# TensorE issues the values of four slots in one block instead of two

## What is computed

```
content  = einsum('bhqd,bhkd->bhqk', q, k)
relative = einsum('bhqd,qkd->bhqk', q, rel_k[idx])      # idx = clip(k - q, -128, 128) + 128
w        = softmax((content + relative) / sqrt(8))
out      = einsum('bhqk,bhkd->bhqd', w, v) + einsum('bhqk,qkd->bhqd', w, rel_v[idx])
x = x + layernorm(out @ Wo.T + bo)
x = x + layernorm(ffn(layernorm(x)))                    # shared expert + the one routed expert
```

## Time and profile before

| | |
|---|---|
| median of three runs | 1906.22 us |
| span of the profiled execution, first to last instruction | 1789.6 us |
| what lies around the span in the median run | 116.6 us |
| TensorE busy | 1620.7 us, 91% of the span |
| TensorE weight loads busy | 1354.0 us, 76% |
| VectorE busy | 1256.6 us, 70% |
| ScalarE busy | 1116.0 us, 62% |
| mean granted TensorE clock | 0.974 |

### The profile page before, as it was taken

One profiled execution on the slowest core, in us unless ns is written; L12 is line 12 of the kernel. 1 busy time (PEld: TensorE's weight loads), 2 busy tenths in 40 slices (PEclk: granted clock), 3 DMA queues, 4 the chain that ended last, 5 costly groups with the idle time before them and its releaser, 6 DMA issues. The chain is left out here.

```text
span 1789.6 us, 72871 instructions
## 1 busy us (share of the span) xinstructions
PE 1620.7 (91%) x28157; PEld 1354.0 (76%) x28157; DVE 1256.6 (70%) x3502; ACT 1116.0 (62%) x2060; POOL 540.0 (30%) x1114
## 2 busy tenths in 40 slices
PE   2889999999999999999999899999999989976991
PEld 1668888888878878887878788888888776555991
DVE  5996658787868776877787768787777234523994
ACT  3337676766766667666766676767656665325880
POOL 5422121413131313131413132313101112770566
PEclk9999999999999999999999999999999999997996
DMA  2478864775454445444544364446433652324451
GB/s 56 128 193 205 171 144 104 172 164 153 90 137 95 124 92 149 78 127 95 153 68 128 80 133 98 117 94 140 95 67 77 151 159 58 123 76 113 140 159 44
DMA packets 490909, 212.47 MB, mean 119 GB/s; under 512 B 332392, under 2 KB 464165, under 8 KB 490561
## 3 DMA queue, kind: packets, MB, share of 16 engines
q1 hardware_dynamic: 475968, 165.76, 41.9%
q0 software_dynamic: 14592, 42.00, 7.1%
HBM read 105.73 MB, written 102.85 MB: 117 GB/s over the span
## 5 line engine op out<-in xcount | busy, mean ns | idle before, releaser
L936 ACT ACTIVATE w<-sc,escale 128x512 f32<-128x512 f32 x1024 | 691.6, 688 | 425.2 <-PE sc L734 271.2
L1137 DVE TENSOR_REDUCE mx<-mix 128x1 f32<-128x512 f32 x960 | 649.0, 686 | 274.0 <-PE mix L713 221.8
L727 PE MATMUL sc<-QC,KC 104*128 104x128 f16 x4096 | 401.0, 221 | 16.1 <-issue 11.8
L753 PE MATMUL pv<-w,VC 128*9 128x128 f32 x8192 | 381.1, 275 | 1.8 <-DVE rel_s L1151 1.8
L727 PEld LDWEIGHTS sc<-QC,KC 104*128 104x128 f16 x4096 | 262.9, 99 | 131.2 <-issue 85.4
L708 PE MATMUL mix<-WE 128*128 128x367 f16 (+2 forms) x960 | 312.0, 325 | 24.4 <-DVE mx L1137 16.2
L709 PE MATMUL mix<-Wn,WE 128*128 128x367 f16 (+2 forms) x960 | 284.5, 296 | 1.1 <-issue 1.1
L927 ACT ACTIVATE WE<-qp,hmask 128x256 f16<-128x256 f16 x512 | 249.4, 501 | 23.9 <-PE sc L711 14.7
L734 PE MATMUL sc<-QT,Wt 96*128 96x64 f16 x5120 | 259.3, 192 | 3.5 <-issue 3.4
L760 PE MATMUL rel<-w,Rv 128*32 128x128 f32 x5120 | 260.6, 274 | 1.7 <-issue 1.7
L753 PEld LDWEIGHTS pv<-w,VC 128*9 128x9 f32 x8192 | 174.7, 90 | 62.2 <-issue 43.6
(11 more groups left out here) (232 smaller groups left out, 2130.3 us busy)
## 6 DMA issues: line engine op xcount, KB each, us to landing
qm_d<-ks POOLq DMA_DIRECT2D x48, 512.0 KB, 4.6
QT<-qm_d SPq DMA_DIRECT2D x32, 768.0 KB
kt_d<-ks SPq DMA_DIRECT2D x48, 256.0 KB
KC<-kt_d SPq DMA_DIRECT2D x128, 96.0 KB
xs_d<-zrow SPq DMA_DIRECT2D x5, 2056.0 KB, 12.1
vs_d<-vst SPq DMA_DIRECT2D x16, 576.0 KB, 5.4
VC<-vs_d SPq DMA_DIRECT2D x32, 288.0 KB
orl_d<-rel_s SPq DMA_DIRECT2D x512, 8.0 KB
```

Of the source, the lines that this page charges most:

```text
L727: mm = nc.tensor.matmul(bank[:, P * g:P * g + P], KC[j][:, b2, g, 0 if near else 1, :], qc[:, g, :, 32 * q8:32 * q8 + 32], start=(g == 0), ...
L753: mm = nc.tensor.matmul(pv[b2][32 * g:32 * g + 9, P * hh:P * hh + P], VC[j][:, b2, 0 if near else 1, h, :], wt[:, :, b2, h, :], start=(j = ...
L936: nc.scalar.activation(w[tile % 2][:, slot % 4, slot // 4 % 2].rearrange("p h q -> p (h q)"), sc[slot % 2][:], ACT.Exp, scale=escale[:, 0: ...
L1137: nc.vector.tensor_reduce(mx[:, k:k + 1], nat[:], AX.X, ALU.max).then_inc(s["mx_done"], 1)
```

## The change

The values of four slots are issued together in every fourth slot (3, 7, 11, ...), where the values of two slots were issued in every second.

```diff
-                if slot % 2 == 1:
-                    for earlier in (slot - 1, slot):
+                if slot % 4 == 3:
+                    for earlier in range(slot - 3, slot + 1):
                         if slot >= 8:
                             values(i, slot // 8 - 1, earlier % 8)
                         elif prev:
                             values(i - 1, 15, earlier)
```

## The result

| | before | after |
|---|---|---|
| median of four runs each, same comparison | 1907.39 us (1903.23 to 1922.66) | 1933.55 us (1931.20 to 1938.91) |
| ratio, 95% interval | | 1.0123 [1.0082, 1.0165] |
| span of a profiled execution on such a chip | 1898.9 us | 1932.5 us |
| the seven turns with sets, first to last | 1270.6 us | 1283.5 us |
| last turn, first scores to last values | 131.1 us | 145.7 us |

The changed kernel is slower by 1.2%, 23 to 26 us. The prediction was 1921 us in a range of 1897 to 1937.

The account below looks back on a forecast made before the run. TensorE was taken to set the pace. The last turn's +11.3 us and the seven turns' +3.5 us (border gains against new waits) sum to +14.8 us, 1921 us by the median, in a range of 1897 to 1937.

Parts of the forecast that it names:

- Border, 0.20 us a block: Entering and leaving each block of values on TensorE costs 0.20 us; 256 fewer blocks, gross gain 5.8 us a turn.
- Last turn, gross +16.0: Without sets to fill the burst, exponentials set the pace; all four kinds of group lengthen, 16.0 us together.
- Last turn, less 4.7 hidden behind DMAs: TensorE's waits for output DMAs at slots 41 and 100 hide 1.8 and 2.9 us, leaving +11.3 us.
- Seven turns, new waits group by group: In turns with sets, work behind slot 0 delays slot 3: gains 3.1, losses 3.6, +0.5 us a turn, +3.5 in seven.
- Slots 92 to 103, -0.6 a turn: VectorE-bound stretch with four reciprocals: its chain starts 1.1 us sooner, 0.5 is lost again behind slot 100.
- The faster one: Rival: borders win, as the seven turns' new waits are half those added up; 1899 us, chance 0.22.
- The rival of no change: Each turn gains 1 us net and DMA waits hide 7.5 us in the last turn; 1908 us, chance 0.24.
- The turn with sets: Sign: a turn with row-maximum sets stays within 1 us of 181; below 179 us the forecast is wrong.
- The other signs: In the new profile: idle by issue ahead of weight loads, L727's and L708's waits, and a last turn of 139 us.

Follow-up runs that it names:

- the two parts: Against the kernel before: fours in the seven turns alone, 1915.58 us, ratio 1.006; fours in the last turn alone, 1918.09 us, ratio 1.0081.
- the 91 groups: Fours in 13 of the 32 groups of each of the seven turns, pairs elsewhere, against the kernel before: 1889.1 us, ratio 0.9904.
- moved work: VectorE's and ScalarE's delaying work put in other slots, against the kernel before: with pairs 1915.46 us, 1.0033; with fours in 27 groups 1901.46 us, 0.9962.
- the last experiment: Fours in 29 of 32 groups of the seven turns, pairs in slots 92 to 103 and the last turn: 1803.72 us, before 1793.22, ratio 1.0067.

## Why the prediction was right, and where it wasn't

The direction and the two mechanisms were right; the size was 9 to 12 us too small: +14.8 forecast, +26.8 by the two parts, +23 to +26 by the whole. The 1933.55 us lie inside the range of 1897 to 1937, but near its upper end.

- **Border, 0.20 us a block.** Holds: 0.21 in plain slots with blocks of one, and 0.21 to 0.23 in the five plainest groups of fours. That the 19.0 us of the 91 groups also come to 0.21 each is in part luck: the interval is 12 to 25 us, or 0.13 to 0.27. The issue idle should have fallen by 64 us and fell by 47 (27 and 20).
- **Last turn, gross +16.0.** Holds. All four kinds of group came within 0.03 us, L727's waits for exponentials grew from 1.6 to 15.4 us, and fours there alone cost 15.4 us (8 to 23). In the three profiles with fours there the turn was longer by 10.7 to 15.8 us.
- **Last turn, less 4.7 hidden behind DMAs.** This is the first step that failed. The waits of the earlier trace rows belong to the chip of the first trace; where the kernels were timed they aren't there, and by the timed medians nothing was hidden (15.4 us for 16.0 forecast gross): about 4 us of the miss. I took one execution for the kernel, though its span (1789.6) and the median (1906.22) couldn't be reconciled but by an unexplained 116.6 us.
- **Seven turns, new waits group by group.** Mostly right. Forecast and measured change (median of the turns of one profile each): slots 16 to 19 +0.45 and +0.45; 20 to 23 +0.55 and +0.64; 52 +0.25 and +0.26; 60 +0.5 and +0.51; 72 +0.45 and +0.43; 84 +0.15 and +0.10; 104 +0.1 and +0.13; 124 +0.75 and +0.75. Too small: 68 (+0.08, +0.26) and 112 (+0.1, +0.25). Too large: 24 (+0.25, -0.06). The list leaves one group out: beside those it names there are 15 and not 14. On the faster chip, where a turn scatters less, the 29 groups outside slots 92 to 103 changed by 1.2 us a turn together (means of seven turns), and 1.1 was forecast.
- **Slots 92 to 103, -0.6 a turn.** This is the second step that failed: the gain isn't there. On the slower chips these slots took 20.41 to 20.93 us a turn in the three profiles with fours there, on average 20.61, and 19.67 to 21.32 in the eight with pairs there, on average 20.47 (20.16 in the five of them without moved work). That is 0.1 to 0.5 us more with fours, less than single profiles with pairs differ by, and in any case no gain of 0.6. Without the 0.6 us the forecast of the seven turns is 7.7 in place of 3.5, inside the interval of what was measured (11.4, 6.9 to 16.0). More can't be laid on these slots: the two kernels with pairs there and fours elsewhere were not faster for it by their medians (1.0134 where all fours had 1.0123, and 1.0067 on the faster chip, where fours in all groups of the seven turns had 1.006 on a slower one).

What the trace after has in these slots is a wait and then a lower clock. TensorE in slot 98:

```profile
820.11 0.38 PE L708 MATMUL mix<-WE 128*128 128x367 f16 x1 [1.09 <-DVE mx L1137]
...
821.51 0.38 PE L708 MATMUL mix<-WE 128*128 128x367 f16 x1 [0.55 <-issue]
...
822.11 0.62 PE L753 MATMUL pv<-w,VC 128*9 128x128 f32 x8
```

And the windows around it (the granted clock is the third number from the end):

```profile
817.29:821.90 4.61, 2.97 (x35) 2.50 (x32) 4.43 (x9) 1.96 (x3) 3.70 (x4) 1.00 0.83 245
821.90:825.30 3.40, 3.40 (x66) 3.01 (x65) 2.97 (x5) 0.69 (x1) 0.40 (x1) 0.50 0.70 236
825.30:830.00 4.70, 4.35 (x53) 3.75 (x49) 3.28 (x6) 3.02 (x5) 0.00 (x0) 1.00 0.18 25
```

Behind a stretch in which TensorE was busy for 2.97 of 4.61 us, the clock is 1.2 GHz in place of 2.4 for 3.4 us, and the four slots of values that were saved up run in it (they take 3.48 us, 822.11 to 825.59, where the group before took 1.87). With fours such a stretch came in these slots in all seven turns of this profile, and in five of seven in each of the other two; with pairs in one to six of seven, by profile. So it doesn't need fours, and where pairs took most of it away (0.5 us a turn in place of 3.3) the kernel was no faster.

- **Rivals.** The faster one needed new waits under 4.2 us a turn; measured they are about 7.4 (5.8 + 11.4/7); the waits that the trace names grew by 5.2 us a turn, also more than that. Its mechanism was real, though, in the groups without extra work: that is the kernel at 0.9904. The rival of no change needed the DMA waits to hide the last turn's loss, and they weren't there.
- **The turn with sets** was to stay within 1 us of 181; its mean went from 181.5 to 183.4, so this sign was wrong by a little.
- **The other signs** came in kind, not all in size: idle by issue ahead of the two weight loads 64.5 and 30.8 us (forecast about 43 and 22), waits of L727 for exponentials 30.3 (about 20) and of L708 for reductions 29.2 (40 or more), the last turn 145.7 us (139, counted over a slightly shorter stretch).

Open: what the rest of the seven turns' loss is (11.4 us on the slower chips, and 12.0 in the last experiment, 7.7 to 16.5, where the list without these slots gives 7.7 and the seven turns of its profile are 9.8 us longer than those of the first trace); and how far the 6.9 us more of the expert layer, whose instructions are the same, is only scatter (362 to 369 us in all twelve profiles on the slower chips, whether with pairs, fours or blocks of one).

## What to carry to other kernels

Grouping work of one kind saves the border, here 0.2 us a block, but the work in between was also what covered the way to another engine and back, here 1.18 us from one scores to the next in the same bank. So decide group by group: fours in 13 of 32 groups gave -1.0%, fours everywhere +1.2%. A stretch whose loop over two banks is closed by another engine (the last turn here) must keep its cover, and moving that engine's work elsewhere helps only if its queue has a free place there. And if the span of a trace and the timed median don't fit, take a second profile before pricing anything by a wait that the first one shows.

## What the runs showed that I hadn't expected

- The same kernel takes 1793 us on one chip and 1903 to 1908 on others. Between the two profiles of the kernel before, 78 us of the 109 are in the expert layer (283.8 and 361.9 us) and 31 in the seven turns; the last turn is equal (131.2 and 131.1). Behind the turns, TensorE of the slower one has a wait that the faster one lacks:

```profile
PE gu L1738 <- issue: 29.7, 5, 7.1
```

- The record of granted clock has 3.4 us stretches at half clock inside dense work, some with no wait of TensorE longer than 0.4 to 1.3 us shortly before them. In the seven turns they come to 27 us in the kernel before and 44 to 54 in the three profiles with fours in all groups, but also to 54 in the profile of pairs with moved work; so that fours bring them isn't shown.
- An exponential of 512 columns takes 0.69 us and one of 128 columns 0.36. The scores behind it came earlier by just that, 0.32 us (0.86 for 1.18 us after the first): the other 0.5 us of the way from scores to exponential and back, the scores' own time among it, stayed.
